# Local attention layers: score products of one head each in 64-row array tiles, two squares moved to ScalarE, and another order of the steps

## The reference

```python
qkv = shift(x) @ Wqkv                      # 128 -> 3 x 1024, 16 heads of 64
q, k = l2norm(q) * qs, l2norm(k) * ksc     # per head
q, k = rotary(q), rotary(k)
sim = einsum('bhwie,bhwje->bhwij', q, [k of the window before, k]) * 8   # windows of 32 tokens
sim = where(mask, -max, sim)               # a query sees itself and the 32 keys before it
x = x + softmax(sim) @ [v before, v] @ Wo
x = x + (a * gelu(gate)) @ W2 + b2         # a, gate = layernorm(shift(x)) * g + b @ W1 + b1, 128 -> 2 x 341
```

## Time and profile before

| | before |
|---|---|
| median of 3 runs | 5763.94 us (5748.97 to 5768.19) |
| profiled execution, its own time | 5774.69 us |
| its span | 5773.4 us |
| TensorE's mean granted clock | 0.937 of 2.4 GHz |
| PE busy | 5193.1 us (90%) |
| DVE busy | 4836.9 us (84%) |
| ACT busy | 3373.3 us (58%) |
| POOL busy | 2898.6 us (50%) |

### The profile page before, as it was taken

How to read it: one execution, slowest core, us unless ns; L and a number is a source line. 1 busy time by engine, 2 the same in 40 slices (tenths; PEclk the granted TensorE clock), 3 DMA queues, 4 the chain that set the end, 5 groups by cost and what they waited for, 6 DMA issues and landing times. The chain is left out here.

```text
span 5773.4 us, 116112 instructions
## 1 busy us (share of the span) xinstructions
PE 5193.1 (90%) x45144; PEld 3092.9 (54%) x45144; DVE 4836.9 (84%) x10806; ACT 3373.3 (58%) x6220; POOL 2898.6 (50%) x3374
## 2 busy tenths in 40 slices
PE   5999996899999999999999999999995999978878
PEld 2333334566656666666666656666663555544445
DVE  5999978999999998999899989999992677757655
ACT  1787883556655665566566656666662466644532
POOL 2121005667766776677667766777671111005534
PEclk6999997999999999999999999999996798978989
DMA  0000002000000000000000000000000000000000
GB/s 21 1 1 1 1 1 66 12 9 9 23 12 9 9 23 12 9 9 23 12 9 9 23 12 8 9 9 12 7 3 24 1 2 2 2 15 1 1 1 15
DMA packets 46646, 61.56 MB, mean 11 GB/s; under 512 B 11260, under 2 KB 33602, under 8 KB 45202
## 3 DMA queue, kind: packets, MB, share of 16 engines
q1 hardware_dynamic: 46098, 54.14, 3.1%
HBM read 25.17 MB, written 4.19 MB: 5 GB/s over the span
## 5 line engine op out<-in xcount | busy, mean ns | idle before, releaser
L1370 POOL TENSOR_TENSOR x<-x,b_norm 128x512 f32<-128x512 f32 x576 | 588.9, 1044 | 610.6 <-DVE b_norm L1238 610.6
L1002 PEld LDWEIGHTS psum<-b_w_vo,b_mixed 128*128 128x128 f32 x6144 | 782.7, 195 | 173.4 <-issue 166.2
L934 PE MATMUL psum<-b_w_qk,b_xst 128*128 128x512 f32 x1536 | 831.0, 623 | 19.7 <-DVE b_cross L1207 17.5
L1002 PE MATMUL psum<-b_w_vo,b_mixed 128*128 128x128 f32 x6144 | 842.9, 281 | 0.0
L588 DVE TENSOR_REDUCE a_top<-psum 128x1 f32<-128x512 f32 x1024 | 637.3, 682 | 90.8 <-PE psum L435 88.5
L538 ACT ACTIVATE a_prob<-psum 128x512 f32<-128x512 f32 x1024 | 556.4, 601 | 137.2 <-PE psum L451 129.2
L1093 ACT ACTIVATE b_prob<-b_prob 128x512 f32<-128x512 f32 x384 | 236.7, 628 | 565.8 <-DVE b_prob L1256 565.6
L1073 ACT ACTIVATE x<-psum 128x512 f32<-128x512 f32 x768 | 462.3, 602 | 116.2 <-DVE b_norm L1215 98.9
L1207 DVE TENSOR_TENSOR b_cross<-psum,b_table 128x512 f32<-128x512 f32 x768 | 520.9, 678 | 0.0
L588 DVE TENSOR_REDUCE c_top<-psum 128x1 f32<-128x512 f32 (+3 forms) x768 | 384.1, 550 | 162.1 <-PE psum L435 159.8
L1361 POOL TENSOR_TENSOR x<-x,b_cross 128x256 f32<-128x256 f32 x576 | 419.7, 729 | 185.8 <-DVE b_cross L1207 185.7
(11 more groups left out here) (320 smaller groups left out, 11231.2 us busy)
## 6 DMA issues: line engine op xcount, KB each, us to landing
b_prev<-b_xs_x SPq DMA_DIRECT2D x24, 384.0 KB, 3.5
b_w_qk<-in_L_ffn_Wqkv SPq DMA_DIRECT2D x6, 1024.0 KB, 7.8
b_shifted_x<-y SPq DMA_DIRECT2D x24, 224.0 KB, 2.5
b_shifted_f<-y SPq DMA_DIRECT2D x24, 224.0 KB, 2.5
b_w_v<-in_L_ffn_Wqkv SPq DMA_DIRECT2D x6, 512.0 KB, 7.6
b_w_o<-in_L_ffn_Wo SPq DMA_DIRECT2D x6, 512.0 KB, 9.6
b_prev<-b_xs_x SPq DMA_DIRECT2D x24, 112.0 KB, 3.3
x<-in_L_attn_x SPq DMA_DIRECT2D x4, 512.0 KB, 6.3
```

What stands on the lines that cost most here:

```text
L934: e.matmul(banks[n], xst_of(l, b)[:, P * t:P * (t + 1)], w_qk[l % 2][:, BANK * c:BANK * (c + 1)], start=True, stop=True).then_inc(filled[n ...
L1002: made = e.matmul(banks[n][:, 0:D], mixed[:, h, :], w_vo[l % 2][:, h, :], start=h == 0, stop=h == 2 * PAIRS - 1)
L1370: e.tensor_tensor(rh, rh, bcast(norm[i % 2][:, 1, HPC * c:HPC * (c + 1)], 2, LDIM), ALU.mult).then_inc(sem["scaled"], 1)
```

## The change

1. `score` becomes one step that fills both banks. Each product takes one head: 64 rows of the array (head `odd` of a pair lies in rows 0 to 63 or 64 to 127), 32 columns, 64 moving columns. Bank 4 takes the even heads and bank 5 the odd ones. The mask goes in by 8 products of 64 rows and 32 columns, one for each array tile. The heads of a bank, and with them the halves of the softmax and the layout of `w_vo`, change from "first eight" and "last eight" to "even" and "odd"; the constant mask of a sequence's first tile is laid out for it.
2. `k_t` has no zeros any more: it is half as large, its memset is gone, and one copy of 128 partitions takes the place of two of 64.
3. Steps 2 and 5 of `invert` and three steps of `norm` (the squares) go from DVE to ACT.
4. The order: PERIOD, all of `PIECES`, `FF_PIECES` and the begins of `norm` and `apply`. `turn_w`, `fold`, `bias`, `place` and `move` keep their times, and so stand elsewhere relative to the rest.

Here cut: the bookkeeping of `slot` for the two banks, the removed "zeroed" semaphore, the removed branch for the squares in `norm_part`, and the line of `mask_constants`.

```diff
-PERIOD = 16.5
+PERIOD = 15.8
...
-NORM_BEGINS, NORM_STEP, APPLY_BEGINS, APPLY_STEP, BIAS_BEGINS = 5.0, 0.6, 0.5, 0.6, 6.0
+NORM_BEGINS, NORM_STEP, APPLY_BEGINS, APPLY_STEP, BIAS_BEGINS = 2.0, 0.55, 2.0, 0.6, 6.0
...
-    project=(0.00, 7.15, 9.81, 13.02), square=(6.78, 10.16, 14.00, 15.07), rope=(9.24, 11.58, 14.77, 15.79),
-    sum_squares=(11.77, 13.85, 14.88, 15.43), add=(14.06, 14.67, 15.61, 20.36), invert=(16.07, 18.01, 18.27, 18.63, 19.53, 22.21, 22.89, 23.14, 23.17),
-    scale=(25.30, 24.63, 26.72, 26.82), turn=(25.58, 25.22, 27.17, 30.47), copy_turned=(26.02, 27.61, 30.04, 32.48),
-    score=(34.49, 35.37), top=(36.90, 39.45), less=(38.11, 40.25), exp=(39.92, 40.43),
-    sum=(40.54, 41.35), invert_sum=(41.30, 42.02), weigh=(42.52, 42.93), block=(43.47, 43.47),
-    gather=(45.47,), spread=(47.66, 48.12, 47.85, 49.99), out=(53.11, 55.58, 56.78, 58.92), join=(60.30,))
+    project=(0.00, 3.34, 7.97, 14.01), square=(1.73, 3.79, 12.67, 15.75), rope=(6.06, 11.25, 15.71, 17.74),
+    sum_squares=(9.59, 15.58, 15.75, 15.90), add=(13.90, 14.09, 15.81, 19.25), invert=(16.64, 16.71, 17.29, 17.99, 18.20, 18.56, 20.40, 20.60, 20.84),
+    scale=(23.17, 25.84, 25.49, 21.55), turn=(23.50, 26.17, 27.21, 30.16), copy_turned=(24.20, 29.34, 31.52, 30.81),
+    score=(33.08,), top=(36.19, 35.98), less=(37.43, 37.49), exp=(38.90, 39.16),
+    sum=(39.25, 41.08), invert_sum=(40.26, 41.54), weigh=(42.06, 45.10), block=(44.49, 46.34),
+    gather=(46.96,), spread=(47.71, 47.96, 47.46, 49.15), out=(49.54, 51.94, 53.60, 55.45), join=(62.15,))
...
-FF_PIECES = dict(fill=(16.43, 21.52, 25.97), empty=(19.27, 25.11, 27.00))
+NORM_SQUARES = range(2 * TILES + 2, NORM_PARTS - 1, 3)
+FF_PIECES = dict(fill=(16.45, 21.44, 26.66), empty=(18.74, 24.10, 29.55))
...
-        k_t, mixed = sb("k_t", [PAIRS, 2, 3, P]), sb("mixed", [2 * PAIRS, P])
+        k_t, mixed = sb("k_t", [PAIRS, 3, P]), sb("mixed", [2 * PAIRS, P])
...
-                    for m in (c, c + 2):
+                    for m in range(4):
                         at, turned = slot["turn", i, m]
                         q.wait_ge(emptied[at], turned)
-                    q.wait_ge(sem["zeroed"], 1)
-                    q.wait_ge(emptied[n], use - 1)
-                    e.matmul(banks[n].rearrange("p (s h k) -> p s h k", s=2, h=HPC), chip.ident_bf[:, :],
-                             bcast(mask.rearrange("p (s k) -> p s k", s=2), 2, HPC),
-                             start=True, stop=False, skip_group_check=True)
-                    heads = banks[n].rearrange("p (s h k) -> p h s k", s=2, h=HPC)
-                    for p in range(4):
+                    for odd in range(2):
+                        n, use = slot["score", i, odd]
+                        half = slice(LDIM * odd, LDIM * (odd + 1))
+                        q.wait_ge(emptied[n], use - 1)
+                        for w in range(WPT):
+                            lo = LDIM * odd + WINDOW * (w > 0)
+                            e.matmul(banks[n][WINDOW * w:WINDOW * (w + 1), :].rearrange("p (s h k) -> p s h k", s=2, h=HPC),
+                                     chip.ident_bf[half, lo:lo + WINDOW],
+                                     bcast(mask[half, :].rearrange("p (s k) -> p s k", s=2), 2, HPC), start=True,
+                                     stop=False, skip_group_check=True, tile_position=(LDIM * odd, WINDOW * w))
+                    for p in range(PAIRS):
                         for w in range(WPT):
                             rows = slice(WINDOW * w, WINDOW * (w + 1))
-                            k = k_t[:, 4 * c + p, :, :, :].rearrange("p h s q -> p h (s q)")
                             lo = P * ks + WINDOW * (w - 1)
...
                             for lo, to in spans:
-                                wide = WINDOW * (to.stop - to.start)
-                                made = e.matmul(heads[rows, 2 * p:2 * p + 2, to, :], qt[:, 4 * c + p, rows],
-                                                k[:, :, lo:lo + wide].rearrange("p h (s q) -> p h s q", q=WINDOW),
-                                                start=False, stop=True, skip_group_check=True,
-                                                tile_position=(0, WINDOW * w))
-                    made.then_inc(filled[n], 1)
+                                for odd in range(2):
+                                    half = slice(LDIM * odd, LDIM * (odd + 1))
+                                    n, use = slot["score", i, odd]
+                                    heads = banks[n].rearrange("p (s h k) -> p h s k", s=2, h=HPC)
+                                    k = k_t[half, p, :, :].rearrange("p s q -> p (s q)")
+                                    wide = WINDOW * (to.stop - to.start)
+                                    made = e.matmul(heads[rows, p, to, :], qt[half, p, rows],
+                                                    k[:, lo:lo + wide].rearrange("p (s q) -> p s q", q=WINDOW),
+                                                    start=False, stop=True, skip_group_check=True,
+                                                    tile_position=(LDIM * odd, WINDOW * w))
+                                    if p == PAIRS - 1 and w == WPT - 1:
+                                        made.then_inc(filled[n], 1)
...
+                if kind == "invert" and step[2] in (2, 5):
+                    q.wait_ge(sem["inverted"], INVERT_PARTS * i + step[2])
+                    e.activation(norm[i % 2][:, 2, :], norm[i % 2][:, 1, :], ACT.Square).then_inc(sem["inverted"], 1)
...
-                    if c < 2:
-                        e.copy(q_t[i % 2][:, pairs, :], by_pair).then_inc(emptied[n], 1)
-                    else:
-                        e.copy(k_t[0:LDIM, pairs, 0, i % 3, :], by_pair[0:LDIM])
-                        e.copy(k_t[LDIM:P, pairs, 1, i % 3, :], by_pair[LDIM:P]).then_inc(emptied[n], 1)
+                    to = q_t[i % 2][:, pairs, :] if c < 2 else k_t[:, pairs, i % 3, :]
+                    e.copy(to, by_pair).then_inc(emptied[n], 1)
...
+                if kind == "norm" and step[3] in NORM_SQUARES:
+                    k = number_of(*step[1:3])
+                    q.wait_ge(sem["norm_parts"], (NORM_PARTS - 1) * k + step[3])
+                    e.activation(chip.spread[:, k % 2, :, 0], chip.spread[:, k % 2, :, 1],
+                                 ACT.Square).then_inc(sem["norm_parts"], 1)
...
-                    elif part in (2, 5):
-                        made = e.tensor_tensor(tmp, root, root, ALU.mult)
...
-                        e.tensor_copy(w_vo[l % 2][:, 8 * c + odd:8 * (c + 1):2, :],
+                        e.tensor_copy(w_vo[l % 2][:, HPC * odd + 4 * c:HPC * odd + 4 * (c + 1), :],
...
-            e.memset(k_t[:], 0.0).then_inc(sem["zeroed"], 1)
```

More of the change, by code:

```diff
@@ L788, in local_stage @@
     single = dict(turn_x=6, turn_f=6, up=6, down=6, out=7)
-    paired = dict(project=0, turn=2, turn_w=2, fold=2, score=4)
+    paired = dict(project=0, turn=2, turn_w=2, fold=2)
     slot = {}
@@ L796, in local_stage @@
                 slot["gather", step[1], w] = 4 + w, chip.fills[4 + w]
+        elif kind == "score":
+            for odd in range(2):
+                chip.fills[4 + odd] += 1
+                slot["score", step[1], odd] = 4 + odd, chip.fills[4 + odd]
         elif kind in paired or kind in single and (kind != "out" or step[2] == 0):
@@ L810, in local_stage @@
     sem = chip.semaphores("b", "dma_small dma_qk0 dma_qk1 dma_vo dma_ff dma_x dma_f dma_prev placed_x placed_f dma_kept "
-                               "table squared summed roped inverted scaled zeroed powered weighed topped totalled norm_parts "
+                               "table squared summed roped inverted scaled powered weighed topped totalled norm_parts "
                                "blocked biased rooted normed gelu cleared entered sums "
@@ L945, in tensor_ @@
                     l, b, t = stream[i]
-                    c = step[2]
                     qt, ks = q_t[i % 2], i % 3
                     mask = opening_mask if t == 0 else window_mask
-                    for m in (c, c + 2):
+                    for m in range(4):
                         at, turned = slot["turn", i, m]
                         q.wait_ge(emptied[at], turned)
-                    q.wait_ge(sem["zeroed"], 1)
-                    q.wait_ge(emptied[n], use - 1)
-                    e.matmul(banks[n].rearrange("p (s h k) -> p s h k", s=2, h=HPC), chip.ident_bf[:, :],
-                             bcast(mask.rearrange("p (s k) -> p s k", s=2), 2, HPC),
-                             start=True, stop=False, skip_group_check=True)
-                    heads = banks[n].rearrange("p (s h k) -> p h s k", s=2, h=HPC)
-                    for p in range(4):
+                    for odd in range(2):
[9 more added lines that the diff above has]
+                    for p in range(PAIRS):
                         for w in range(WPT):
```

(21 more changed lines are left out.)

1 line of the change is left out of this document (removed).

## The result

The changed kernel takes 5688.7 us (median of 4 runs, 5677.77 to 5705.57) against 5764.94 us for the kernel before beside it: ratio 0.9876, 95% interval 0.9845 to 0.9907. That is 76 us less where 184 were forecast. The profiled execution took 5685.46 us with a span of 5683.9.

A forecast was written before the change was run, and what follows sets the result against it. It took PE (94%) and DVE (93%) as both full in stage B. DVE's terms, -163 + 35 - 3 - 35 - 20 = -186 us, with PE letting all pass, gave 5580 us, range 5510 to 5690.

The forecast's parts named there:

- under 10 ns for an instruction: PE's score step: products are priced by columns, with under 10 ns for each instruction of its own.
- rival 5: Each score product has a price of its own: step 3.9 us, kernel slower at 5950 us; chance 0.07.
- rival 2: The array's row halves take turns: score step 2.66 us, total 5705 us; chance 0.12.
- rival 4: ACT's squares stall DVE, 0.5 us x 384 = +192: 5770 us, no change; chance 0.06.
- Term (b): DVE's waits for POOL's `add` move: step 4 +96 us, integer step -61, net +35.
- I take side by side, 1.32 us: PE's new score step: both row halves of the array work at once, so masks and products take 1.32 us.
- Slack 0.9, if the score step holds its price: From `block` 1 to `top` 1: `gather`, `spread`, `score` take 4.9 us, covered by 5.8 us of DVE steps.
- (d): DVE's waits for PE before the `turn_w` and `fold` copies, 71 us: half saved, -35 us.
- (c): `norm` squares leave DVE, 49.6 us, against trips to ACT, +24, and a later `bias`, +29: net about -3 us.
- (e): DVE's named stalls at `weigh` and `square`, 0.45 us in a tile, 86 us in all: -20 us taken.
- The -105 for all of the waiting being paid again: Sum for the `invert` squares and moved POOL waits on DVE if all waiting returned, where the forecast had -128 us.
- (a): Both `invert` squares leave DVE: 151.3 us busy and 12 us of gaps, -163 us.

The follow-up runs named there:

- e3: Kernel before with only the new score step and `k_t`, old order, squares on DVE: 5813.6 us, ratio 1.0084.
- e5: Changed kernel with all squares back on DVE, in the new order: 5759.76 us, ratio 1.0001 to the kernel before.
- e4: Kernel before with the two `invert` squares on ACT and `apply` moved later, old score step: 5712.71 us, ratio 0.9914.
- e7: Changed kernel with half as many score products, each 128 columns wide (every second pair's scores wrong): 5573.04 us, ratio 0.9662 to the kernel before.
- e12: e7 with its mask products written three times, to make the step as long as the changed kernel's: 5601.28 us, ratio 0.9715 to the kernel before.
- e8: Changed kernel with POOL's `bias` at 3.6 instead of 6.0, before the first `scale`: 5653.62 us, ratio 0.9793 to the kernel before.
- e1: Changed kernel with the score step in two halves and an `out` step between them: 5800.67 us, ratio 1.0076 to the kernel before.
- e11: e10 with the score step in two halves and the first `fill` step between them: 5621.72 us, ratio 0.9756 to the kernel before.
- e10: e8 with `score` ahead of the first `fill` step and the odd `spread` copy first: 5688.97 us, ratio 0.9858 to the kernel before.

## Why the prediction was off

**Right.** Two full engines, though "relief of one alone is worth little" holds in part only: relief of PE brought nothing (e3, e5, both with their stops), relief of DVE alone 49 us (e4). DVE's work at 2969 us (2990 forecast). Some tiles are as short as forecast, but not the ordinary one: from one `block` step to the next, 66 of 191 intervals are at most 15.8 us, and the median is 16.98 (before 16.78, in e7 16.18). The price of a product: 32 more cost 0.29 us (1.91 − 1.62), 9 ns; 64 fewer 0.36 us (e7), 6 ns; "under 10 ns for an instruction" holds, and with it rival 5 falls. So does rival 2 (2.7 us for the step), and rival 4: DVE waits 2 us in all for the `invert` squares and 7 for those of `norm`. Term (b): step 4 went from 0.252 us in the mean (0.191 at the median) to 0.711, +88 where +96 was said; the integer step from 0.638 to 0.215, −81 where −61 was said; so +7 net where +35 was said.

The Trainium skill ("TensorE: Matmul & The Clock Gate", section "Wait — 56ns, not 53.3ns?") has starts no closer than about 25 ns. The trace disagrees for products that lie in different array tiles: 128 of them start within 1.39 us (2011.87 to 2013.26), 11 ns each, across row groups too. The Trainium skill ("SBUF — State Buffer", section "Who interferes with whom") has DVE and GpSimd share a port pair under an exclusive lock. The trace agrees: 0.71 us for a 128x32 step behind `add`, where the median before was 0.19.

**The step that failed** is PE's part, "I take side by side, 1.32 us", with the sentence that closes the sum, "PE, relieved by 1.41 x 192 = 271, lets all of it pass". It priced the instructions by the time that the array takes, and not by what it takes to bring them. The step is 1.62 or 1.91 us, 0.38 more in the mean, and in 51 tiles it stops for 2.0 us more, each time where a packet of instructions ends. e12 against the changed kernel puts the stops at some 87 us (by the ends of the two intervals 67 to 118), e7 against e12 the longer step at some 28. Without either, e7 comes to 5573 where 5580 was forecast; that it is so close is in part luck, since smaller terms were off both ways (below). The number of instructions had been seen ("what speaks against it"), but only as a price each, and the sum had no term for their supply.

**Second, the slack.** "Slack 0.9, if the score step holds its price": it had hardly any. DVE waits for the score step 117 times, more than twice as often as there are stops; in e12, with one stop, still 87 times, and 36 times in e7 with its shorter step. One such wait, in a tile without a stop:

```profile
2043.82 1.29 DVE L1262 TENSOR_REDUCE b_stat<-psum 128x8 f32<-128x512 f32 x2 [0.54 <-PE psum L983]
```

With slack of 0.9, a stop of 2.0 would have cost 1.1. Why the slack is missing in those tiles isn't shown; a sum of durations over a loop leaves out, for one, that the PE queue may be busy with a `fill` step just then.

**Third, smaller terms.** (d) The two waits of `turn_w` and `fold` went from 71 to 61 us, not by 35. (c) `bias` was given 29 us; moving it gave back 35 (e8), so the place was right and the size near. But the sum of (c) is wrong: -49.6 + 24 + 29 is +3 and not -3. (e) The two kinds of wait weren't in every tile as in the one read: over the stage they were 44 us and not 86, and are 36 now. The -105 for all of the waiting being paid again doesn't follow from its figures either: with the 81 us back, (a) is -82. (a) −163 was right as work, but as time the squares are worth 71 us (e5) or, alone in the old order, 49 (e4, 0.86%): 151 us of their busy time were 81 of waiting for POOL, and part of that is paid again at step 4. The terms don't add up to the 109 us of the miss, since the engines cover for each other.

**Open.** The boundary tells which steps can stop, but of the 44 in which it comes after 191 to 245 records 20 stop and 24 don't; when a packet is asked for, the runs don't say. That halves with work between them stop for a shorter time (e1, e11) and steps of 176 to 208 instructions all but never do (e12) fits a supply that is fetched ahead by some amount, but the amount wasn't measured. Nor was it tried to load fewer weights for the same products, to pack products by another layout that keeps all scores right, or to move the boundaries.

## What to carry to other kernels

Splitting matmuls into small array tiles is paid in instructions as well as in columns: count the instructions of a dense stretch, loads included, and look in the trace for stops by "issue" with a packet of the instruction queue just ahead, and for their distances in instructions, which here are multiples of 256. When two engines are full, price an edit only together with its order: the same score step cost 48 us in one order and brought 130 in another, and some 87 us were lost to short stops that no share of busy time shows. Where a dense stretch can't be avoided, work put into it shortens the stops; it paid with work that the same engine owed anyway (a `fill` step, e11: 67 us less than e10) and not with work that made the waiting engine later (e1: 112 us more).

## What the hardware showed unexpectedly

- PE runs out of instructions. The instruction queue moves 16.4 KB packets, 256 of PE's records each, and every stop in the changed kernel's score steps stands where one ends: steps of 272 to 336 instructions in 1.6 to 1.9 us stopped 51 times for 2.0 us, in e12, steps of 176 in 1.73 us (208 where it has 80 products) stopped once, and in e7, steps of 144 in 1.26 us (176) never. PE went on no sooner than 1.2 us after the packet had landed.
- Eight array tiles of 64 rows and 32 columns work side by side: 128 products of 64 columns in 1.39 us, and the first product starts 0.23 us after the first of eight mask products of 512 columns.
- DVE's wait for POOL's instruction was handed on by the new order, not removed: the 128x32 step that stands behind `add` takes 0.71 us, the integer step before, step 4 after.
